# One transfer to all 128 partitions in place of two or four to parts of them, for every copy of x

## The reference

```python
# ids: (1024, 32); 32 tables of width 16; W0: (128, 1024); W1, W2: (128, 2048)
e = stack([tbl_f[ids[:, f]] for f in range(32)], axis=1)       # x: 1024 x 32 fields x 16
def cin(x, Ws, bs):
    h, xs = x, []
    for i in range(3):
        z = (x[:, :, None, :] * h[:, None, :, :]).reshape(B, F * G, E)   # every field by every row of h
        y = relu(einsum('oc,bce->boe', Ws[i], z) + bs[i][None, :, None])
        if i != 2: x_keep, h = y[:, :64], y[:, 64:]
        else:      x_keep = y
        xs.append(x_keep)
    return sum(concatenate(xs, axis=1), axis=2)                # 1024 x 256
h = maximum(concatenate([cin(e, ...), dense_ctx], 1) @ W_top1 + b_top1, 0)
y = maximum(h @ W_top2 + b_top2, 0) @ W_top3                   # 1024 x 1
```

## Time and profile before

| | us |
|---|---|
| median of 3 runs | 1115.0 (1112.3 to 1119.1) |
| profiled execution, from the first to the last instruction (its span) | 1109.1 |
| DVE busy | 987.2 (89%) |
| PE busy | 994.0 (90%) |
| POOL busy | 882.4 (80%) |
| ACT busy | 572.7 (52%) |
| SP's transfers, share of the 16 DMA engines' time | 76.8% |

### The profile page before, as it was taken

One profiled execution on the slowest core, in us unless ns is written; L12 is line 12 of the kernel. 1 busy time (PEld: TensorE's weight loads), 2 busy tenths in 40 slices (PEclk: granted clock), 3 DMA queues, 4 the chain that ended last, 5 costly groups with the idle time before them and its releaser, 6 DMA issues.

```text
span 1109.1 us, 12343 instructions
## 1 busy us (share of the span) xinstructions
PE 994.0 (90%) x3281; PEld 611.0 (55%) x3281; DVE 987.2 (89%) x842; ACT 572.7 (52%) x683; POOL 882.4 (80%) x525
## 2 busy tenths in 40 slices
PE   3167989998997979999899989999899999999988
PEld 2134556564654646555556656555556656565665
DVE  6246999999996999999999999999999999999982
ACT  0234556554654545565555645565455556555553
POOL 7645899997977979997999979997999966665760
PEclk9588999998998999999899999999899999999999
DMA  6199989899886869898888879888788989888500
GB/s 118 14 195 198 184 170 190 195 186 191 168 192 133 164 163 199 175 194 177 168 183 182 195 174 193 184 186 190 156 182 179 192 194 191 185 197 193 124 1 1
DMA packets 111813, 184.55 MB, mean 166 GB/s; under 512 B 19570, under 2 KB 24178, under 8 KB 111540
## 3 DMA queue, kind: packets, MB, share of 16 engines
q1 hardware_dynamic: 103604, 182.24, 76.8%
q0 software_dynamic: 8192, 2.11, 1.9%
HBM read 181.15 MB, written 3.15 MB: 166 GB/s over the span
## 4 chain that ended last, share of the span: by engine, by line
POOL 29%; DVE 18%; issue 18%; DMA 15%; PE 13%; ACT 4%; SPq 2%; DVEq 1%; POOLq 0%; ACTq 0%
POOL low L490 15%; POOL looked_up L480 12%; DVE unsplit L1043 9%; DMA xcols<-xrows 6%; PE y L604 6%; DMA shifted<-xcols 5%; DVE prod L1043 4%; PE y L612 4%; PE y L627 2%; POOL tail_parts L498 2%; DMA spread<-xcols 1%; SPq L390 1%; DMA looked_up<-in_tbl,ids_now 1%; ACT h L794 1%; DVE tail L1025 1%
## 5 line engine op out<-in xcount | busy, mean ns | idle before, releaser
L490 POOL TENSOR_TENSOR low<-unsplit,high 128x1024 fp32r<-128x1024 f32 x222 | 543.7, 2454 | 110.5 <-ACT high L808 108.3
L808 ACT CAST high<-unsplit 128x1024 fp32r<-128x1024 f32 x320 | 334.0, 1047 | 330.2 <-DVE unsplit L1043 322.7
L604 PE MATMUL y<-prod,w1T 128*128 128x512 f32 x1024 | 491.4, 609 | 5.1 <-ACT kept L800 2.7
L480 POOL DMA_INDIRECT looked_up<-in_tbl,ids_now x256 | 291.3, 1138 | 69.3 <-issue 58.6
L1043 DVE TENSOR_TENSOR prod<-spread,h 128x1024 f32<-128x1024 f32 x256 | 307.1, 1210 | 7.9 <-ACT h L794 7.4
L1043 DVE TENSOR_TENSOR unsplit<-spread,h 128x1024 f32<-128x1024 f32 x256 | 307.7, 1212 | 4.2 <-ACT h L794 4.2
L604 PEld LDWEIGHTS y<-prod,w1T 128*128 128x128 f32 x1024 | 196.0, 195 | 171.1 <-issue 149.5
L627 PE MATMUL y<-low,w2T_high 128*128 128x512 f32 x512 | 222.5, 518 | 48.4 <-POOL low L490 47.5
L612 PE MATMUL y<-high,w2T_high 128*128 128x512 f32 x512 | 217.1, 424 | 5.7 <-ACT high L808 5.5
L1051 DVE TENSOR_TENSOR low<-unsplit,high 128x1024 fp32r<-128x1024 f32 x98 | 187.3, 1911 | 22.3 <-ACT high L808 22.3
L612 PE MATMUL y<-high,w2T_low 128*128 128x512 f32 x512 | 202.9, 396 | 0.0
(11 more groups left out here) (114 smaller groups left out, 482.4 us busy)
## 6 DMA issues: line engine op xcount, KB each, us to landing
spread<-xcols SPq DMA_DIRECT2D x256, 512.0 KB, 6.9
shifted<-xcols SPq DMA_DIRECT2D x124, 256.0 KB, 4.6
shifted_tail<-xcols SPq DMA_DIRECT2D x124, 64.0 KB, 4.9
looked_up<-in_tbl,ids_now POOLq DMA_INDIRECT x256
xcols<-xrows SPq DMA_DIRECT2D x32, 96.0 KB, 5.5
spread<-in_L_rec_W SPq DMA_DIRECT2D x3, 512.0 KB, 7.1
spread<-in_L_rec_W SPq DMA_DIRECT2D x1, 1024.0 KB, 10.9
wt<-in_W_top SPq DMA_DIRECT2D x2, 512.0 KB, 9.4
```

The source lines that it names most:

```text
L480: pool.indirect_dma_start(out=looked_up[:, f, :], out_offset=None, in_=tables[f][:, :], in_offset=bass.IndirectOffsetOnAxis(ap=ids_now[:, ...
L490: pool.tensor_tensor(low[kind][r][:, :, :], unsplit[kind][r][:, :, :], high[kind][r][:, :, :].bitcast(F32), ALU.subtract).then_inc(s_low[k ...
L604: last = pe.matmul(y[:, :], w1T[:, ITEM * n + c, :], z[:, c, :], start=(n == 0 and c == 0), stop=(item == LAST1 and c == ITEM - 1))
L808: act.copy(high[kind][r][:, :, :], unsplit[kind][r][:, :, :]).then_inc(s_high[kind], 1)
```

## The change

All copies are now brought by one transfer each. To make every partition's share contiguous, x is stored twice: `xcols` as before, and `xpairs`, 32 rows in which the 16 even fields come first and then the 16 odd ones. Four consecutive rows (8 KB) of `xpairs` are then what one partition of a group of `spread` needs, and four consecutive rows of `xcols` what one partition of `shifted` needs. SP waits for both stores together. As chunk a of layer 0 now holds other bands than before, the reordering of its weights (`w0_dist`) and of the first tile's rows (`rotated`) changes with it; one copy of 480 columns becomes four of 128.

```diff
                 sp.dma_start(xcols[number(t)], xrows[:, :]).then_inc(s_xcols, 16)
-                sp.wait_ge(s_xcols, 16 * (number(t) + 1))
+                pairs = xpairs[number(t)]
+                sp.dma_start(bass.AP(pairs.tensor, pairs.offset,
+                                     [[COLS, FIELDS // 2], [FIELDS // 2 * COLS, 2], [1, COLS]]),
+                             xrows[0:FIELDS, :]).then_inc(s_xcols, 16)
+
+                sp.wait_ge(s_xcols, 32 * (number(t) + 1))
...
-                for j in range(GROUP):
-                    sp.dma_start(shifted[FIELDS * j:FIELDS * (j + 1), :, :],
-                                 bass.AP(x.tensor, x.offset + j * COLS,
-                                         [[COLS, FIELDS], [GROUP * COLS, GROUP], [1, COLS]])
-                                 ).then_inc(s_shifted, 16)
-                for j in range(GROUP):
-                    sp.dma_start(shifted_tail[FIELDS * j:FIELDS * (j + 1), :],
-                                 x[FIELDS // 2:XROWS, :]).then_inc(s_shifted_tail, 16)
+                sp.dma_start(shifted[:, :, :],
+                             bass.AP(x.tensor, x.offset,
+                                     [[GROUP * COLS, GROUP], [COLS, FIELDS], [1, GROUP * COLS]])
+                             ).then_inc(s_shifted, 16)
+                sp.dma_start(shifted_tail[:, :],
+                             bass.AP(x.tensor, x.offset + FIELDS // 2 * COLS,
+                                     [[0, GROUP], [COLS, FIELDS], [1, COLS]])).then_inc(s_shifted_tail, 16)
...
-                for half in range(2):
-                    sp.dma_start(spread[k % 2][HALF * half:HALF * (half + 1), GROUP * g:GROUP * (g + 1), :],
-                                 bass.AP(x.tensor, x.offset + (2 * GROUP * g + half) * COLS,
-                                         [[0, HALF], [2 * COLS, GROUP], [1, COLS]])
-                                 ).then_inc(s_spread[k % 2][g], 16)
+                sp.dma_start(spread[k % 2][:, GROUP * g:GROUP * (g + 1), :],
+                             bass.AP(x.tensor, x.offset + GROUP * g * COLS,
+                                     [[FIELDS // 2 * COLS, 2], [0, HALF], [1, GROUP * COLS]])
+                             ).then_inc(s_spread[k % 2][g], 16)
...
-            dve.tensor_copy(w0_dist[:, FIELDS:FIELDS * H].rearrange("p (d f) -> p d f", f=FIELDS),
-                            bass.AP(w0_wide.tensor, w0_wide.offset + 1,
-                                    [list(w0_wide.ap[0]), [1, H - 1], [2 * FIELDS + 1, FIELDS]])).then_inc(s_sym, 1)
+            for a in range(GROUP):
+
+                dve.tensor_copy(w0_dist[:, P * a:P * (a + 1)].rearrange("p (j f) -> p j f", f=FIELDS),
+                                bass.AP(w0_wide.tensor, w0_wide.offset + a,
+                                        [list(w0_wide.ap[0]), [GROUP, GROUP], [2 * FIELDS + 1, FIELDS]])).then_inc(s_sym, 1)
...
-                                bass.AP(unwrapped.tensor, unwrapped.offset + GROUP * c,
-                                        [list(unwrapped.ap[0]), [XROWS, QUAD], [1 if c < GROUP else 0, GROUP], [1, FIELDS]])
+                                bass.AP(unwrapped.tensor, unwrapped.offset + (c if c < GROUP else FIELDS // 2),
+                                        [list(unwrapped.ap[0]), [XROWS, QUAD], [GROUP if c < GROUP else 0, GROUP], [1, FIELDS]])
```

More of the change, by code:

```diff
@@ L162, in dlrm_tower @@
 def dlrm_tower(nc, dense_ctx, ids, tables, w_top1, b_top1, w_top2, b_top2, w_top3,
-               w0, b0, w1, b1, w2, b2, xcols, out):
+               w0, b0, w1, b1, w2, b2, xcols, xpairs, out):
     batch = ids.shape[0]
@@ L388, in load_shifted @@
                     return
-                for j in range(GROUP):
-                    sp.dma_start(shifted[FIELDS * j:FIELDS * (j + 1), :, :],
-                                 bass.AP(x.tensor, x.offset + j * COLS,
-                                         [[COLS, FIELDS], [GROUP * COLS, GROUP], [1, COLS]])
-                                 ).then_inc(s_shifted, 16)
-                for j in range(GROUP):
-                    sp.dma_start(shifted_tail[FIELDS * j:FIELDS * (j + 1), :],
-                                 x[FIELDS // 2:XROWS, :]).then_inc(s_shifted_tail, 16)
+                sp.dma_start(shifted[:, :, :],
[5 more added lines that the diff above has]
+                                     [[0, GROUP], [COLS, FIELDS], [1, COLS]])).then_inc(s_shifted_tail, 16)
             def load_spread(t, g):
-                x = xcols[number(t)]
+                x = xpairs[number(t)]
                 k = t[1]
@@ L549, in _ @@
             pe.wait_ge(s_ident, 1)
-            pe.wait_ge(s_sym, 7)
+            pe.wait_ge(s_sym, 10)
             turn(0, GROUP, P, lambda c: w0_dist[:, P * c:P * (c + 1)])
@@ L785, in take_x @@
                 act.wait_ge(s_xT, number(t) + 1)
-                act.wait_ge(s_xcols, 16 * number(t))
+                act.wait_ge(s_xcols, 32 * number(t))
                 act.copy(xrows[:, :], xT[0:XROWS, :]).then_inc(s_xrows, 1)
@@ L876, in top_high @@
                     act.wait_ge(s_xT, TILES)
-                    act.wait_ge(s_xcols, 16 * TILES)
+                    act.wait_ge(s_xcols, 32 * TILES)
                     copy = act.copy(wt2_high[:, :], wt2[:, :])
@@ L939, in _ @@
             H = FIELDS // 2
-            dve.tensor_copy(w0_dist[:, FIELDS:FIELDS * H].rearrange("p (d f) -> p d f", f=FIELDS),
-                            bass.AP(w0_wide.tensor, w0_wide.offset + 1,
-                                    [list(w0_wide.ap[0]), [1, H - 1], [2 * FIELDS + 1, FIELDS]])).then_inc(s_sym, 1)
+            for a in range(GROUP):
+                dve.tensor_copy(w0_dist[:, P * a:P * (a + 1)].rearrange("p (j f) -> p j f", f=FIELDS),
+                                bass.AP(w0_wide.tensor, w0_wide.offset + a,
+                                        [list(w0_wide.ap[0]), [GROUP, GROUP], [2 * FIELDS + 1, FIELDS]])).then_inc(s_sym, 1)
+            dve.wait_ge(s_sym, 3)
             dve.tensor_copy(w0_dist[:, 0:FIELDS], diagonal(w0_raw, FIELDS, 0, FIELDS)).then_inc(s_sym, 1)
@@ L947, in _ @@
                             diagonal(w0_raw, FIELDS, H * FIELDS, H)).then_inc(s_sym, 1)
-            dve.wait_ge(s_sym, 6)
+            dve.wait_ge(s_sym, 9)
             once = w0_dist[:, FIELDS * H:FIELDS * (H + 1)]
@@ L1016, in multiply @@
                 elif item == (0, 0):
-                    dve.wait_ge(s_shifted, 16 * GROUP * number(t))
+                    dve.wait_ge(s_shifted, 16 * number(t))
                 if item == (0, 0):
@@ L1021, in multiply @@
                     if not isinstance(t[0], int) or number(t) > 0:
-                        dve.wait_ge(s_shifted_tail, 16 * GROUP * number(t))
+                        dve.wait_ge(s_shifted_tail, 16 * number(t))
                     dve.wait_ge(s_tail_low, number(t))
@@ L1032, in multiply @@
                     if n % (GROUP // ITEM) == 0:
-                        dve.wait_ge(s_spread[t[1] % 2][n // (GROUP // ITEM)], 32 * uses_of_parity(t))
+                        dve.wait_ge(s_spread[t[1] % 2][n // (GROUP // ITEM)], 16 * uses_of_parity(t))
                 if item == (2, 0):
@@ L1194 @@
     xcols = nc.dram_tensor("xcols", (tiles, XROWS, COLS), F32, kind="Internal").ap()
+    xpairs = nc.dram_tensor("xpairs", (tiles, FIELDS, COLS), F32, kind="Internal").ap()
     out = nc.dram_tensor("out", (batch, 1), F32, kind="ExternalOutput").ap()
@@ L1197 @@
                dram("W_top2"), dram("b_top2"), dram("W_top3"), dram("L0_rec_W0"), dram("L0_rec_b0"),
-               dram("L0_rec_W1"), dram("L0_rec_b1"), dram("L0_rec_W2"), dram("L0_rec_b2"), xcols, out)
+               dram("L0_rec_W1"), dram("L0_rec_b1"), dram("L0_rec_W2"), dram("L0_rec_b2"), xcols, xpairs, out)
     result = run_bass_kernel_spmd(nc, [arrays], core_ids=[0])
```

## The result

The changed kernel takes 3344.4 us (median of 4 runs, 3339.5 to 3348.5), the kernel before 1117.1 us in the same comparison: a ratio of 2.991, 95% interval 2.980 to 3.002. The span of its profiled execution is 3338.9 us.

A forecast was written before the change was run, and what follows sets the result against it. DVE was taken to bound the kernel, transfers close behind. After the change the busiest engine's packets (`spread` 2703, `shifted` 327, tail 82), stores 13, lookups 21, gaps 93, start 56 and end 60 make 3355, forecast as 3360 us; range 3050 to 4550.

The forecast's parts named there:

- The number of engines: SP's new transfers: the smaller outermost count of both sides decides, so 2 engines for `spread`, 4 for `shifted` and its tail.
- The packet of `spread`: 8 KB piece to 128 partitions: 0.33 us; on the busiest engine 32 tiles x 4 groups x 64 packets, 2703 us.
- The packet of `shifted`: 8 KB piece, also 0.33 us; on the busiest engine 31 tiles x 32 packets, 327 us.
- an 8 KB packet well over 0.33 us: Sign in the profile after: if an engine's 8 KB packet takes this long, the prediction is wrong.
- The tile: One pass of the tile loop: about 102 us in place of 30.9.
- the gap, the tail, stores and lookups: Per tile on the busiest engine: 3 us between store and `shifted`, 2.6 for `shifted_tail`, 0.4 for stores, 0.7 for lookups.
- Start and end: Before the first `spread` packets run, 56 us; from item (1, 6) of slot 31 to the end, 60 us.
- DVE's waits: DVE waits for transfers some 70 us per tile, some 2200 in all, mostly before (1, 0), (1, 2), (1, 6), (0, 0).
- the longest single wait: On DVE, the longest wait was to be for `spread`.
- The rivals: Three other outcomes for the new transfers, 18% together: about 1085 us (8%), about 1113 us (4%), about 5720 us (6%).
- The small edits: SP's 8 issues per tile for 17, DVE's four copies for one (0 to 0.8 us), changed wait counts: taken as nothing.
- The faster rival: All 16 engines carry the new transfers, 8 KB in 0.33 us in place of 0.60; about 1085 us; chance 8%.

The follow-up runs named there:

- the series: Changed kernel with `shifted` and tail in parts, `spread` still one transfer, its source given 2, 4, 8, 16 outermost steps: 2922.3, 1829.7, 1566.9, 1116.4 us.
- run 2: Not a run: in "its packets run 2 us later" the word is a verb and 2 us a time, so there is no change or measurement to give.
- all_parts: Changed kernel with `spread` cut into halves, `shifted` and its tail into four parts, 8 KB pieces and both stores kept: 1115.1 us, 1.0044 of the kernel before.
- flat128: Changed kernel with `spread` as one transfer whose source has 128 outermost rows (step 0), `shifted` and tail in four parts: 1108.3 us, 0.9966 of the kernel before.

## Why the prediction was right

- **The number of engines**, the step on which all hangs, held: 2 for `spread` and 4 for `shifted`, by the closing packets of the series and by the shares of 12.6% and 25.4%. The earlier trace rows were enough to see that the outermost dimension counts; that the smaller side decides was an argument there and is now shown.
- **The packet of `spread`**: 0.33 us forecast, 0.315 measured, so 8192 x 0.015 = 123 us too much.
- **The packet of `shifted`**: 0.33 us forecast, 0.54 measured. 120 packets in 16 us make 17.1 us for the 128 of a transfer, where I had 10.6: 31 x 6.5 = 202 us too little. The prediction names an 8 KB packet well over 0.33 us as a sign of being wrong, and for `shifted` that sign came. This is the term that was mis-sized, and the prediction had the reason in its hands: the earlier trace rows showed 0.58 us beside 0.34, I put it down to 64 against 128 partitions, and did not ask which partitions 4 engines would write.
- **The tile**: 101.4 us, 101.8 forecast. 256 x 0.315 = 80.6 and 17.1 leave 3.7 us for the gap, the tail, stores and lookups, where I had 6.7: 31 x 3.0 = 93 us too much. The three errors, 123 - 202 + 93, nearly cancel; that 3360 us came so close to 3344 is in good part luck. The split between the last two is rough: it is from one slot, where `shifted` took 20.6 us from issue to DVE, and the mean of all 31 is 18.7. Their sum, 109 us too little, is from the tile's 101.4 us and holds.
- **Start and end**: 56 and 60 us forecast. SP issues the first `spread` at 54.97 us, and its packets run 2 us later; (1, 6) of slot 31 begins at 3276.18, 62.7 us before the end.
- **DVE's waits**: 2366 us for these transfers, 2200 forecast. The item (0, 0) was named among the four, but the longest single wait was forecast for `spread`, and it is 37.1 us for `shifted`, with 1069 us in all.
- **The rivals.** The small edits, the second store and the 8 KB pieces all remain in all_parts and cost 5 us together there, so "nothing" was about right. The faster rival's mechanism exists (flat128, where the share fell to 0.59), but its price was wrong: 4 us against the kernel before, 7 against all_parts, and not 30. I had taken DVE's 31.00 busy us in 31 as DVE's own work and the wait for `shifted` as time that would be won.

No version here beats the kernel before with both halves of x in their places: flat128 gives all partitions the same half, and wins only 0.3% with that.

## What to carry to other kernels

Write down both sides of a transfer as lists of steps, and look at the first count of each: the smaller one, up to 16, was the number of DMA engines that worked in every case here, all of them powers of two. A repeat or a split by halves belongs behind a dimension of 16 or more, even if that makes two transfers of one. When transfers wait but the DMA share is low, divide the share into engines (12.6% of 16 is 2) before thinking of bandwidth. And when the share is high, ask whether pairs of engines write the same partitions, as bytes per engine-us tell (8 KB in 0.315 or in 0.58 us here, 26 or 14 KB).

## What was not expected of the hardware

- SP itself is held up when the engines are behind. The instruction that issues the store of `xcols` took 19.32 us at 1386.89 in the changed kernel, against 0.35 us in the earlier trace rows. Of the 55.72 us of the four of `spread` before it, 16.13 and 27.90 us lie in the issues, and 11.5 between them wait for DVE:

```profile
1330.91 16.13 SPq L409 DMA_DIRECT2D spread<-xpairs  x2
...
1358.74 27.90 SPq L409 DMA_DIRECT2D spread<-xpairs  x2
...
SPq L409 <- DVE unsplit L1050: 17.3, 2, 11.5
```

- DVE's busy time fell from 987.2 to 895.7 us with the same multiplications to do; 63 of these 91 us are the 98 subtractions of `low`, 1.91 us each before and 1.27 after.
- Twice the engines can be little gain: 6.4 packets of 8 KB per us with 2 engines (`spread`) and 7.5 with 4 (`shifted`). By the time of a packet, 8 engines on partitions of their own would move 8 / 0.315 = 25 per us and 16 in pairs 16 / 0.585 = 27; this is an estimate, as DVE sets the pace in both.
